# Opening of a two-stage attention and tree kernel: both halves of x measured first, TensorE given transposes before its first work, later weights loaded early, nine steps in other slots

## The reference

```python
x = x + attn_a(layernorm(x))      # 16 heads of 16, q, k, v and output with biases
x = x + ffn(layernorm(x))
x = x + attn_b(layernorm(x))      # rotary, causal, no biases
x = x + ffn(layernorm(x))

def ffn(x):                       # a soft binary tree of depth 8
    gate = sigmoid((x @ Wq.T) @ routers.T)            # 255 nodes
    leaf_prob = product of gate or 1 - gate down to each of 256 leaves
    return (leaf_prob @ leaf_values) @ Wout_w.T + Wout_b
```

## Time and profile before

| what | value |
|---|---|
| time of the profiled execution | 1141.19 us |
| its span | 1139.5 us |
| TensorE busy | 1075.6 us (94%) |
| VectorE busy | 883.5 us (78%) |
| ScalarE busy | 761.6 us (67%) |
| GpSimd busy | 307.0 us (27%) |
| granted TensorE clock, mean | 0.99 |

### The profile page before, as it was taken

How to read it: one execution, slowest core, us unless ns; L and a number is a source line. 1 busy time by engine, 2 the same in 40 slices (tenths; PEclk the granted TensorE clock), 3 DMA queues, 4 the chain that set the end, 5 groups by cost and what they waited for, 6 DMA issues and landing times.

```text
span 1139.5 us, 18953 instructions
## 1 busy us (share of the span) xinstructions
PE 1075.6 (94%) x6164; PEld 543.1 (48%) x6164; DVE 883.5 (78%) x2481; ACT 761.6 (67%) x1565; POOL 307.0 (27%) x339
## 2 busy tenths in 40 slices
PE   5899999999999999999999999999999898989986
PEld 3323444444445444554455544454444555545544
DVE  4887787787868897687977878788886878777844
ACT  3577767677776678765777767776776666666562
POOL 3011110114213150222403151131513526262210
PEclk9999999999999999999999999999999999999999
DMA  8150501402205131321305023051311313022001
GB/s 240 49 128 19 130 20 50 99 20 85 83 20 130 38 107 43 99 70 38 111 20 149 20 66 102 19 131 35 103 50 40 110 38 122 28 85 65 20 20 37
DMA packets 79778, 80.97 MB, mean 71 GB/s; under 512 B 13088, under 2 KB 68672, under 8 KB 79680
## 3 DMA queue, kind: packets, MB, share of 16 engines
q1 hardware_dynamic: 79616, 79.73, 24.6%
q0 software_dynamic: 64, 0.03, 0.0%
HBM read 20.71 MB, written 8.39 MB: 26 GB/s over the span
## 4 chain that ended last, share of the span: by engine, by line
PE 59%; DVE 22%; ACT 7%; issue 4%; SPq 3%; POOL 2%; DMA 1%; POOLq 0%; DVEq 0%; ACTq 0%
PE ps_work L1304 13%; PE ps_out L1213 12%; PE ps_max L1167 11%; PE ps_key L1189 11%; DVE neg_max L916 8%; PE ps_work L1343 7%; ACT probs L797 4%; PE ps_work L1269 3%; DVE scratch L1073 3%; DVE ps_max L912 2%; SPq L538 2%; DVE scratch L1103 2%; DVE scratch L1076 2%; ACT turned_block L818 2%; DVE moments L1021 1%
## 5 line engine op out<-in xcount | busy, mean ns | idle before, releaser
L797 ACT ACTIVATE probs<-ps_key 128x512 f32<-128x512 f32 (+3 forms) x1024 | 515.4, 520 | 297.2 <-PE ps_key L1189 291.5
L916 DVE TENSOR_REDUCE neg_max<-ps_max 128x1 bf16<-128x512 f32 x512 | 336.9, 684 | 86.5 <-PE ps_max L1167 85.2
L1167 PE MATMUL ps_max<-k_stack,q_stack 96*128 96x512 bf16 (+3 forms) x1024 | 347.0, 345 | 24.0 <-DVE neg_max L912 10.0
L1189 PE MATMUL ps_key<-q_stack,k_stack 97*128 97x512 bf16 (+3 forms) x1024 | 348.4, 343 | 16.0 <-ACT probs L797 10.5
L912 DVE CUSTOM_DVE_ANT_0 ps_max<-ps_max,mask_b 128x128 f32<-128x128 f32 (+3 forms) x512 | 247.1, 504 | 105.5 <-PE ps_max L1167 102.7
L1213 PE MATMUL ps_out<-probs,v_ones 128*32 128x512 f32 (+3 forms) x2048 | 233.8, 529 | 0.6 <-POOL probs L688 0.6
L1167 PEld LDWEIGHTS ps_max<-k_stack,q_stack 96*128 96x128 bf16 x1024 | 99.4, 97 | 277.1 <-DVE neg_max L916 109.8
L688 POOL TENSOR_SCALAR_AFFINE_SELECT probs<-probs 128x512 f32<-128x512 f32 x128 | 82.2, 643 | 402.3 <-ACT probs L797 401.7
L1189 PEld LDWEIGHTS ps_key<-q_stack,k_stack 97*128 97x128 bf16 x1024 | 100.9, 99 | 139.7 <-ACT probs L797 87.6
L1213 PEld LDWEIGHTS ps_out<-probs,v_ones 128*32 128x32 f32 x2048 | 40.4, 108 | 73.7 <-issue 65.3
L912 DVE DVE_READ_ACCUMULATOR2_ANT neg_max<- 128x1 bf16 x512 | 72.8, 142 | 0.0
(11 more groups left out here) (93 smaller groups left out, 1254.1 us busy)
## 6 DMA issues: line engine op xcount, KB each, us to landing
k_stack<-k_part SPq DMA_DIRECT2D x108, 128.0 KB, 2.4
q_stack<-q_part SPq DMA_DIRECT2D x108, 128.0 KB, 2.4
k_stack<-k_part SPq DMA_DIRECT2D x42, 256.0 KB
q_stack<-q_part SPq DMA_DIRECT2D x42, 256.0 KB
x_in<-in_x SPq DMA_DIRECT2D x8, 512.0 KB, 3.9
q_stack<-shift_rows SPq DMA_DIRECT2D x256, 1.0 KB, 1.7
x_again<-in_x SPq DMA_DIRECT2D x8, 512.0 KB, 3.9
spill<-x_plain SPq DMA_DIRECT2D x8, 512.0 KB, 2.8
```

The costliest lines, as they stand in the source:

```text
L797: act.activation(probs[step % RING][:, j, q0:T], ps_key[slot % 2][:, 0:T - q0], ACT.Exp, scale=SCALE).then_inc(on["exp_done"], 1)
L916: dve.tensor_reduce(out=dst, in_=src, axis=AX_X, op=ALU.max, negate=True)\
L1167: pe.matmul(dst[:, 0:keys], q_stack[n % 2][0:SPLIT_ROWS, h, P * qt:P * qt + P], k_stack[n % 2][0:SPLIT_ROWS, h, 0:keys], start=True, stop= ...
L1189: pe.matmul(ps_key[slot % 2][:, 0:T - q0], k_stack[n % 2][0:STACK_ROWS, h, P * kb:P * kb + P], q_stack[n % 2][0:STACK_ROWS, h, q0:T], star ...
```

## The change

The change has five parts.

1. In the opening both halves of x are measured before either is normalized. `normalize` waits for the factor of its own half only, and its four instructions then stand together.
2. TensorE no longer waits for the first weights at its start but at its first projection. A new step `awake` has it transpose the identity 24 times before the first real transposes, 4 times between them and 6 times after them, into `ps_out`, which nobody reads then. ScalarE does a small exponential on constants at its start, which loads its table, and waits for the first weights at its first projection.
3. The weights `REST` are issued by SyncE right behind `FOLD`, ahead of the next x.
4. `values` stands before `fold` in the list. Of `fold`, VectorE scales the two gate halves first, then adds the two leaf halves; the scaling of the leaves becomes a step of its own, in slot 40 of phase 0, and the first `mix` waits for it. The opening waits for the gate halves alone.
5. Nine rows of the tables name other slots: in `FINISH_IN_PLAIN` turn_attended 1 one slot later, gates 1 one slot earlier, leaves 0 and 1 one slot earlier; in `PREPARE_PLAIN` moments 0 three slots earlier, high_k 1 and rest_q 1 one later, middle_q 1 three later; in `PREPARE_CAUSAL` the second part of heads_q 0 on TensorE one later.

```diff
 FINISH_IN_PLAIN = (
-    ("turn_attended", 1, (14,), 15), ("project_out", 0, (18, 19), 20), ("moments", 0, (), 21),
+    ("turn_attended", 1, (15,), 16), ("project_out", 0, (18, 19), 20), ("moments", 0, (), 21),
...
-    ("turn_block", 1, (31,), 32), ("gates", 0, (35, 37), 38), ("gates", 1, (38, 39), 40), ("leaves", 0, (), 42),
-    ("leaves", 1, (), 43), ("leaves", 2, (), 44), ("leaves", 3, (), 45), ("leaves", 4, (), 46),
+    ("turn_block", 1, (31,), 32), ("gates", 0, (35, 37), 38), ("gates", 1, (37, 38), 39), ("leaves", 0, (), 41),
+    ("leaves", 1, (), 42), ("leaves", 2, (), 44), ("leaves", 3, (), 45), ("leaves", 4, (), 46),
...
 PREPARE_FIRST = (
-    ("moments", 0, 0), ("spread", 0, 0), ("normalize", 0, 0), ("normalize", 1, 0), ("moments", 1, 0), ("spread", 1, 0),
-    ("normalize", 2, 0), ("normalize", 3, 0), ("load_second", 0, 0), ("turn_normed", 0, 0), ("turn_normed", 1, 0),
+    ("moments", 0, 0), ("spread", 0, 0), ("moments", 1, 0), ("spread", 1, 0), ("normalize", 0, 0), ("normalize", 1, 0),
+    ("normalize", 2, 0), ("normalize", 3, 0), ("load_second", 0, 0), ("awake", 0, 0), ("turn_normed", 0, 0),
+    ("awake", 1, 0), ("turn_normed", 1, 0), ("awake", 2, 0),
...
-    ("middle_k", 1, 0), ("middle_q", 1, 0), ("low_k", 1, 0),
+    ("middle_k", 1, 0), ("middle_q", 1, 0), ("values", 0, 0), ("values", 1, 0), ("low_k", 1, 0),
...
-    ("fold", 0, 0), ("values", 0, 0), ("values", 1, 0),
+    ("fold", 0, 0),
 )
+AWAKE = (24, 4, 6)
...
     if n == 0:
+        yield (), 40, "scale", 0, 0
...
             def load_second(m, i, n, bank):
                 load_x(1)
-                for name in REST:
-                    load_weight(sp, name, rest_loaded)
...
             for name in FOLD:
                 load_weight(sp, name, fold_loaded)
+            for name in REST:
+                load_weight(sp, name, rest_loaded)
...
-            act.wait_ge(first_loaded, DMA * len(FIRST))
+            act.wait_ge(zeroed, 3)
+            act.activation(table_row[:, :], minus_half[:, :], ACT.Exp)
...
-                dve.wait_ge(on["rstd"], count.of("rstd"))
+                dve.wait_ge(on["rstd"], count.of("rstd", 1 - t // 2))
...
-                pe.wait_ge(folded, KC + 1)
+                pe.wait_ge(folded, KC)
...
+            def awake(m, i, n, bank, parts):
+
+                for _ in range(AWAKE[i]):
+                    pe.transpose(ps_out[:, 0:P], ident[:, :], ident[:, :])
```

29 lines of the change are left out of this document (20 added, 9 removed).

## The result

The changed kernel took 1138.73 us (median of 7 runs, 1133.58 to 1139.81) beside 1144.03 us of the kernel before (7 runs, 1141.09 to 1146.10). The ratio is 0.9944 with a 95% interval of [0.9925, 0.9962], so 6.4 us less, between 4.3 and 8.6. In a second comparison on another chip it was 0.9949 [0.9931, 0.9967]. Over all runs of this study whose clock is on record, the mean of the 84 of the kernel before is 1142.3 us and that of the 19 of the changed kernel 1137.3: 5.0 +- 1.2 us less. The profiled execution took 1136.95 us with a span of 1135.2 (before 1141.19 and 1139.5): 4.3 us less.

What follows compares the result with a forecast made beforehand. TensorE, busy 94% of the span, was taken to bound the kernel, with an uncovered opening until 31.02 us. Opening 5.0 plus tables 6.0 made 11.0 us off 1144.35: 1133.4 us, own range 1129 to 1137.5, stated range 1128.5 to 1141.5.

Steps and rivals of the forecast that it cites:

- First maximum at 26.0: Opening: VectorE's first running maximum starts at 26.0 us instead of 31.02, a gain of 5.0 us passed on to phase 0.
- hidden, by 2 us: Opening: the first half's twelve stack transfers, issued by 21.0 us, land at 23.4 and hold nothing up.
- closer: Opening: the next x, needed at 18.8 us, lands at about 17.5, a smaller margin than for other loads.
- Clock: Opening: the 34 added transposes bring TensorE to full clock before the first projections, gaining 2.5 us.
- The rival: Opening: transposes do not raise the clock, so the opening gains only 0.7 us; time 1137.7 us, chance 0.22.
- Tables, forecast 6.0: Moved table rows: 3.7 + 0.8 + 1.5 = 6.0 us less, bounds 0.5 and 10.
- Slots 41 to 48: Seven plain finishing phases: earlier gates and leaves save 1.1 us in phases 1 and 2 each, 0.3 in the others; 3.7 us.
- I take one of the two held instructions as freed: Slots 41 to 48: one of two VectorE leaf instructions slowed beside GpSimd's bias additions runs free; 1.1 us in phases 1 and 2 each.
- Half clock: Phase 1: the 3.4 us at half clock after the long wait may go if that wait shrinks; 0.8 us.
- Slots 14 to 17: Nine phases: moving one ScalarE copy later removes TensorE's 0.36 us wait for an exponential; half counted, 9 x 0.17 = 1.5 us.
- waits only move: Tables: freed slots are handed to the next wait, so tables give only 1.0 us; time 1138.4 us, chance 0.17.
- Slower by an overrun of VectorE at slots 42 to 46: All seven plain finishing phases: each pays up to one held leaf instruction, 1.2 us, 8.4 in all; time 1147.8 us, chance 0.05.

Runs made afterwards that it cites:

- e6: Changed kernel with the later weights issued only behind all stack transfers of the opening; 1136.89 us, ratio 0.9948 to the kernel before.
- e7: Changed kernel with the reload of x for the residual issued at slot 30 instead of 40; 1142.60 us, ratio 0.9996 to the kernel before.
- e9: Changed kernel with the second part of heads_q 0 of causal elements back in slot 7; 1135.96 us, ratio 0.9937 to the kernel before.

## Why the prediction was right, and where it was wrong

**First maximum at 26.0: TensorE's own path right to 0.5 us, one step failed.** First projection 10.4 forecast, 10.60 measured. Projections at full clock from their start: yes. Values and fold to 24.6 forecast; in e6, where nothing else is in the way, 25.08. Gate halves 0.8 forecast, 0.75. In e6 the two additions for the leaf sum (0.51 us) still stand ahead of the first maximum on VectorE, but beside the first score, and it starts at 26.43. Of the forecast 5.0 us the first profile of the changed kernel has 4.46; that was a good draw, since of the six only this one lies within the 26.0 +- 0.7 that was to show it, and against 31.02 they gain 2.3 to 4.5, 3.7 in the middle. The runs have 2 to 3.

The failed step is "hidden, by 2 us". It took the twelve as issued at 21.0 us (21.87, because the first part was there at 14.08 and not 13.7, and twelve issues took 7.8 us and not 7.3) and added 2.4 us to landing, a number from a page that averages over the whole program. In the opening the queues are full: there the medians are 3.9 to 5.4 us, and the transfer that the first score waits for took 4.6 to 6.6. It was there at 25.9 to 28.1 us, not at 23.4; in e6 it was, at 23.75. That made SyncE's queue and the landing the end of the chain. The prediction had named this transfer as "what could be late next", and the price was 0.1 to 2.3 us, 0.9 in the middle.

The next x was called "closer", due at 18.8 us and reckoned there at 17.5 from 5 MB and the rate of the opening. It landed at 18.97 in the first profile, just in time, and at 19.75 to 21.30 in the other five, where VectorE waited 0.65 to 2.05 us for it. That reckoning was short by 1.5 to 3.8 us. What the wait costs was not measured apart from that for the stack transfers.

**Clock: right.** 2.5 us forecast for it. Without the transposes the first maximum is 2.2 us later than in e6, where no transfer is in the way, and 1.3 later than in the middle of the six profiles of the changed opening; the runs give 2.7 +- 1.1. The rival had a chance of 0.22 and a time of 1137.7 us, near the measured one: the time alone would have spoken for a mechanism that the weight loads exclude.

**Tables, forecast 6.0: the larger step that failed.** Its terms:
- Slots 41 to 48, 3.7 forecast: 1.5 in the profiles (0.6 to 0.8 in each of phases 1 and 2, nothing in the other five). "I take one of the two held instructions as freed" did not hold. Two were held before, and two are held after, larger ones; the rule of the Trainium skill that stood beside it (SBUF — State Buffer, Who interferes with whom) described this, since the 2.5 us of GpSimd meet whatever VectorE does then. And the wait was not one for the held instruction alone: with none of the large ones held (e7) TensorE still waited 1.3 us in two places.
- Half clock, 0.8 forecast: not shown. The stretch is not tied to the wait: of the ten profiles with the moved leaf rows five have one in phase 1 or 2, of the three with the old rows two. The mean clock of the runs rose from 0.9886 to 0.9902, worth 1.1 +- 1.1 us by the slope; what raised it is open.
- Slots 14 to 17, 9 x 0.17 = 1.5 forecast: 1.8 in the four causal phases, 0.45 each, and nothing in the plain ones. The sum was right by two errors; no run took these rows back alone, so that the 1.8 is theirs rests on the wait of 0.32 us at slot 18 of phase 6, which is there with the old rows and gone with the new. In the plain phases the wait for an exponential (slot 17 to 18) went, but the second turned copy came one slot later and the output projection then waited for it, 0.3 us, and 0.3 more stands at slot 47 (0.70 where 0.41 was). Timeline of TensorE, phase 5, slot 18 of the changed kernel, where the earlier trace rows had 0.36 us of waiting ahead of the first of these lines:

```profile
407.93 0.39 PE L1204 MATMUL ps_key<-q_stack,k_stack 97*128 97x512 bf16 x1
...
408.42 1.13 PE L1324 MATMUL ps_work<-b_o,turned_block 128*128 128x256 f32 x4
```

- heads_q 0, 0 forecast: with the old row (e9) nothing moved that could be told.

So the tables brought 3.3 us in phases 1 to 11 at full clock, against 6.0, and 0 to 2 in the runs. In phases 12 to 14 they brought and cost nothing that shows: there each phase has a place that the prediction did not look at, slot 35, where TensorE waits for SyncE's transfers with old rows and new. The rival "waits only move", with 0.17, had tables at 1.0 and 1138.4 us; what happened lies between it and the forecast, and its mechanism is what slots 14 to 18 and 41 to 48 show. That the measured 1138.73 is so near its time is partly luck, since the opening gave less than the 5.0 it counted. "Slower by an overrun of VectorE at slots 42 to 46" did not happen: no plain phase was over 0.4 us longer at full clock.

**The base.** The forecast started from 1144.35 us, the median of three runs; the median of the 84 later ones is 1141.7. From that base the same gain would have given 1130.7, 8 us from the measured time and not 5.3. The gain is what was forecast too high, 11.0 against 5.0 +- 1.2.

**What stays open.** Opening and tables apart give -2.0 +- 1.1 us at equal clock, together -3.9 +- 0.8 (-5.0 +- 1.2 by the plain means), and by the profiles (3.7 in the middle, and 3.3) more than either; the leaf steps taken back cost the runs 2.5 and the phases 1.3. One profile per kernel is not enough to split 2 us in a program whose clock alone moves it by 6.

## What to carry to other kernels

Give a cold TensorE throwaway transposes while the first load is under way; it costs nothing where the engine waits anyway, and here bought 2.2 us in the profiles and 2.7 +- 1.1 in the runs. A load that is issued earlier on a queue delays the small transfers behind it: price those with the landing time of that stretch, not with the page's median, and put the large load behind them where its own due time allows. Where TensorE is busy for 97% of a phase, a step moved by one slot mostly moves a wait; look first at what the next wait on each engine is, and compare phases only at equal clock. Profile an opening more than once before a number rests on it.
